# The inverse transforms of two neighbouring tiles, done in a row every second round of the last stage

## The chip, the cores and the metric

The kernel runs on one core of a Trainium2 chip. The metric is the device time of one execution in microseconds. The engines are TensorE (PE in the rows, its weight loads PEld), VectorE (DVE), ScalarE (ACT), GpSimd (POOL) and SyncE (SP), which here only issues transfers.

## What is computed

A block of two layers over x of shape 8 x 2048 x 512, in float32:

```python
proj = (layernorm(x) @ in_proj_w + in_proj_b).reshape(B, L, C, 3)
v, x_branches = proj[..., 0], [proj[..., 1], proj[..., 2]]
v = depthwise_conv3(v) + short_b
h = gelu(gelu(pos @ fw1 + fb1) @ fw2 + fb2)
coefs = (h @ fw3 + fb3).reshape(L, C, 2)
for i in range(2):                       # only the last pass reaches the output
    conv = irfft(rfft(v, n=2*L) * rfft(coefs[..., i], n=2*L))[:L]
    output = x_branches[i] * conv
x = x + output @ out_w + out_b
x = x + layernorm(x) @ (sum_k weights[k] * W[ids[k]]).T + bias
```

The transforms run as products with constant matrices.

## The kernel before

Four stages follow one another: prep builds the filter's first transform step, front does the first layer norm, the projections and the first transform step of each batch, middle the inner transforms and the product with the filter's spectrum, and back the rest. The change is in back, which runs from near 1512 us to the end.

back handles 128 tiles of 128 rows by 512 channels: 8 batches (b) of 16 tiles (t). For each tile TensorE does

- conv: the last inverse step, `psC` from `fin` (loaded from spec3) and the constant `s4`. It is two float32 matmuls, h = 0 and 1, each with 64 output columns of weights, written to the lower and the upper half of psC's partitions. The trace has two records (passes) for each, so four a tile.
- turn_o: four transposes of o into `psP`.
- project: 12 matmuls into `psO` (high and low parts of o times out_w).
- turn_z: four transposes of the normalised rows z into `psT`.
- adapt: 12 matmuls into `psF` (high and low parts of z times the mixed adapter).

VectorE does gate (psC plus a correction, then times the gate, giving `o`), o_low (low part of o), residual (`y` = psO + x, bn_stats, bn_aggr), z_low, finish (psF + yb) and bias_x (out_b added to x). ScalarE makes the high parts and the norm, GpSimd the norm's scalars, `yb` and the correction `corr` in two operations (L1170, L1172). SyncE issues the loads: load_conv, load_gate, load_x.

The order is written by hand with the helper pipelined: each engine has a list of (step, lag), and in round s it runs, in the order of the list, each step for tile s - lag. Rounds run over all tiles of all batches; the first 5 and the last 5 are not full. TensorE's list is [(conv, 1), (adapt, 5), (turn_o, 1), (turn_z, 4), (project, 2)], VectorE's is [(residual, 3), (gate, 1), (finish, 5), (o_low, 1), (z_low, 4), (bias_x, 0)], GpSimd's [(scalars, 3), (bias_y, 3), (correct, 0)], ScalarE's [(norm, 3), (o_high, 1), (z_high, 4), (store, 6)], SyncE's all have lag 0. A tile's conv at lag 1 therefore runs in the same round as its gate, its turn_o and its o_low.

Of the waits that matter here: conv of tile t waits for fin's load and for gate's sum of tile t-2 (psC has two buffers, by t % 2); load_conv of tile t waits for conv of t-2; gate waits for corr and for conv; turn_o for o, and for o_low of the tile before (psP has one buffer); adapt for z_low of the round before; residual for project's psO.

Of the kernel before, what the change touches and what calls it, by code (L numbers as in the profile page):

```python
# [14 lines left out]
B = 8  # L15
# [6 lines left out]
T = 16  # L22
# [110 lines left out]
def pipelined(eng, outer, tiles, stages):  # L133

    fill = max(lag for _, lag in stages)

    def step(i, s, last):
        for stage, lag in stages:
            t = s - lag
            if t >= tiles and not last:  # L140
                stage(i + 1, t - tiles)
            elif 0 <= t < tiles:
                stage(i, t)

    for s in range(fill):
        step(0, s, False)

    def one_pass(i, last):
        for s in range(fill, tiles + fill):
            step(i, s, last)  # L150

    one_pass(0, False)
    with eng.Fori(1, outer - 1) as i:
        one_pass(i, False)
    one_pass(outer - 1, True)


def old(b, t, n):

    return not (isinstance(b, int) and b * T + t < n)  # L160


def hyena_adapter_kernel(nc, x, in_w, in_b, short_w, short_b, fw1, fb1, fw2, fb2, fw3, fb3,
# [14 lines left out]
    def mm3(pe, out_ps, w_hi, w_lo, d_hi, d_lo, first, last):  # L178

        pe.matmul(out_ps, w_hi, d_hi, start=first, stop=False)  # L180
        pe.matmul(out_ps, w_hi, d_lo, start=False, stop=False)  # L181
        return pe.matmul(out_ps, w_lo, d_hi, start=False, stop=last)  # L182
# [861 lines left out]
    def back(bc):  # L1044
        with ExitStack() as st:
# [68 lines left out]
            def no(b, t):  # L1114
                return b * T + t

            @block.sync
            def _(sp):
                def load_edges(b, t):
                    if not (isinstance(b, int) and b == 0):  # L1120
                        return
                    for q in range(2):
                        sp.dma_start(edge[:, q, t], edge_f[q][:, t * C:(t + 1) * C]).then_inc(edge_in[t], 16)  # L1123

                def load_conv(b, t):
                    if old(b, t, 2):
                        sp.wait_ge(c_ps, no(b, t) - 1)
                    sp.dma_start(fin[:, t % 2], spec3[b].rearrange("(r h t) c -> t r h c", h=2, t=T)[t]).then_inc(f_in[t % 2], 16)

                def load_gate(b, t):  # L1130
                    if old(b, t, 2):
                        sp.wait_ge(o_done, no(b, t) - 1)
                    sp.dma_start(gin[:, t % 2], gate_d[b, t // SUB].rearrange("p (s c) -> s p c", s=SUB)[t % SUB]).then_inc(g_in[t % 2], 16)

                def load_x(b, t):
                    if old(b, t, D):
                        sp.wait_ge(y_done, no(b, t) - D + 1)
                    for h in range(2):
                        sp.dma_start(xin[h * N1:(h + 1) * N1, t % D], by_tile(x[b])[h, :, t]).then_inc(x_in[t % D], 16)  # L1139

                pipelined(sp, B, T, [(load_conv, 0), (load_edges, 0), (load_gate, 0), (load_x, 0)])
# [70 lines left out]
            @block.tensor  # L1212
            def _(pe):
                def conv(b, t):
                    pe.wait_ge(f_in[t % 2], 16 * (b * (T // 2) + t // 2 + 1))
                    if old(b, t, 2):
                        pe.wait_ge(a_done, no(b, t) - 1)
                    for h in range(2):
                        mm = pe.matmul(psC[t % 2][h * N1:(h + 1) * N1, :], s4[:, h * T + t, :], fin[:, t % 2, h, :], start=True, stop=True)  # L1219
                    mm.then_inc(c_ps, 1)  # L1220

                def turn_o(b, t):
                    pe.wait_ge(o_done, no(b, t) + 1)
                    if old(b, t, 1):
                        pe.wait_ge(o_lo, no(b, t))
                    for ct in range(CT):
                        mm = pe.transpose(psP[:, ct * P:(ct + 1) * P], o[:, t % 2, ct * P:(ct + 1) * P], ident[:])  # L1227
                    mm.then_inc(p_ps, 1)

                def project(b, t):  # L1230
                    pe.wait_ge(o_lo, no(b, t) + 1)
                    if old(b, t, 2):
                        pe.wait_ge(y_done, no(b, t) - 1)
                    for ct in range(CT):
                        mm = mm3(pe, psO[t % 2][:], oh[:, t % 2, ct * P:(ct + 1) * P], ol[:, t % 2, ct * P:(ct + 1) * P],
                                 woh[:, ct], wol[:, ct], ct == 0, ct == CT - 1)
                    mm.then_inc(o_ps, 1)

                def turn_z(b, t):
                    pe.wait_ge(z_done, no(b, t) + 1)  # L1240
                    if old(b, t, 1):
                        pe.wait_ge(z_lo, no(b, t))
                    for ct in range(CT):
                        mm = pe.transpose(psT[:, ct * P:(ct + 1) * P], z[:, t % 2, ct * P:(ct + 1) * P], ident[:])  # L1244
                    mm.then_inc(t_ps, 1)

                def adapt(b, t):
                    pe.wait_ge(z_lo, no(b, t) + 1)
                    if old(b, t, 2):
                        pe.wait_ge(res_done, no(b, t) - 1)  # L1250
                    for ct in range(CT):
                        mm = mm3(pe, psF[t % 2][:], zh[:, t % 2, ct * P:(ct + 1) * P], zl[:, t % 2, ct * P:(ct + 1) * P],
                                 wfh[:, ct], wfl[:, ct], ct == 0, ct == CT - 1)
                    mm.then_inc(ff_ps, 1)

                pipelined(pe, B, T, [(conv, 1), (adapt, 5), (turn_o, 1), (turn_z, 4), (project, 2)])

            @block.vector
            def _(dve):
# [100 lines left out]
```

## Time and profile before

| what | us |
|---|---|
| median of 3 runs | 2512.56 (2511.91 to 2514.34) |
| the profiled execution | 2518.87 |
| its span, first to last instruction | 2516.8 |
| TensorE busy in the span | 2386.8 (95%) |
| VectorE busy | 1556.8 (62%) |
| GpSimd busy | 914.8 (36%) |
| ScalarE busy | 847.5 (34%) |
| mean granted clock of TensorE | 0.977 of 2.4 GHz |

Shares of the span are averages over stages with different limits. In the last stage, from 1512 us on, TensorE's digits are at 9 tenths or more and VectorE's at 8. Matmuls are pipelined and the ends of their records are modelled, so starts say more than ends: the distance from one start to the next is what a matmul takes in the flow.

### The profile page before, as it was taken

How to read it: one execution, taken by the hardware profiler on the slowest of the kernel's cores; microseconds unless marked ns; L12 is line 12 of the kernel's file. 1: busy time of each engine (PE TensorE's matmuls, PEld its weight loads, DVE VectorE, ACT ScalarE, POOL GpSimd, SP SyncE). 2: the span in 40 equal slices, each digit the busy share in tenths (PEclk: the TensorE clock that was granted, in tenths of full speed). 3: DMA queues.
4: the chain of work that ended last, by engine and by line, in shares of the span. 5: the costliest groups of instructions: out<-in, count | busy, mean ns of one | idle time of the engine just before them, and what ended most of it. 6: DMA issues, size and time to landing. Idle time of an engine off the chain costs nothing. (4 is left out here: it accounts for less than half of the span.)

```text
span 2516.8 us, 39567 instructions
## 1 busy us (share of the span) xinstructions
PE 2386.8 (95%) x12804; PEld 1573.6 (63%) x12804; DVE 1556.8 (62%) x2188; ACT 847.5 (34%) x1151; POOL 914.8 (36%) x1189
## 2 busy tenths in 40 slices
PE   6689999999999999779999987999999999999998
PEld 2257777777777777533333335777777777777776
DVE  6734444443444444257666765788888888888885
ACT  3333344344443344234444441222222222222222
POOL 2322222222222222100000005666666666666664
PEclk9889999999999999889999998999999999999999
DMA  5534435444354435489999987755555555555553
GB/s 188 201 127 151 155 134 190 164 154 168 136 188 150 154 133 191 167 323 346 338 336 339 345 308 236 233 176 171 169 175 175 170 170 174 175 168 170 175 176 94
DMA packets 207925, 496.59 MB, mean 197 GB/s; under 512 B 18411, under 2 KB 18732, under 8 KB 190836
## 3 DMA queue, kind: packets, MB, share of 16 engines
q1 hardware_dynamic: 153588, 395.09, 48.3%
q10 hardware_dynamic: 54272, 100.68, 10.9%
q8 instruction: 35, 0.57, 0.1%
q14 instruction: 30, 0.25, 0.0%
HBM read 276.27 MB, written 219.43 MB: 197 GB/s over the span
## 5 line engine op out<-in xcount | busy, mean ns | idle before, releaser
L1034 DVE TENSOR_TENSOR m_m<-m_psA,m_spec 128x1024 f32<-128x1024 f32 x256 | 295.4, 1217 | 151.9 <-PE m_psA L939 148.4
L1194 ACT ACTIVATE b_z<-b_y,b_shift,b_rstd 128x512 f32<-128x512 f32 x128 | 104.5, 816 | 712.5 <-POOL b_shift L1161 712.5
L701 POOL TENSOR_TENSOR vl<-v,vh 128x512 fp32r<-128x512 f32 x128 | 165.6, 1294 | 433.2 <-ACT vh L661 433.2
L956 PE MATMUL m_psW<-m_m,mats 64*64 64x512 f32 x2048 | 248.6, 592 | 0.0
L939 PE MATMUL m_psA<-m_xin,mats 64*64 64x512 f32 x1536 | 203.3, 604 | 44.6 <-DMA m_xin<-spec 33.8
L180 PE MATMUL b_psF<-wfh,b_zh 128*128 128x512 f32 x512 | 216.3, 423 | 3.4 <-DVE b_zl L1297 3.4
L180 PE MATMUL psV<-wvh,nth 128*128 128x512 f32 x512 | 215.8, 421 | 0.0
L790 DVE TENSOR_TENSOR gto<-psG,bgr 128x512 f32<-128x512 f32 x128 | 87.5, 683 | 204.2 <-PE psG L182 204.2
L180 PE MATMUL b_psO<-woh,b_oh 128*128 128x512 f32 x512 | 212.8, 416 | 0.0
L180 PE MATMUL psG<-wgh,nth 128*128 128x512 f32 x512 | 204.3, 399 | 0.0
L182 PE MATMUL b_psF<-wfh,b_zl 128*128 128x512 f32 x512 | 202.8, 396 | 0.0
L181 PE MATMUL b_psF<-wfl,b_zh 128*128 128x512 f32 x512 | 202.4, 395 | 0.0
L669 ACT ACTIVATE fs1o<-psS 128x1024 f32<-128x1024 f32 x128 | 131.7, 1029 | 209.1 <-PE psS L743 209.1
L182 PE MATMUL psG<-wgh,ntl 128*128 128x512 f32 x512 | 202.1, 395 | 0.0
L181 PE MATMUL psV<-wvl,nth 128*128 128x512 f32 x512 | 201.9, 394 | 0.0
L182 PE MATMUL psV<-wvh,ntl 128*128 128x512 f32 x512 | 201.7, 394 | 0.0
L182 PE MATMUL b_psO<-woh,b_ol 128*128 128x512 f32 x512 | 201.2, 393 | 0.0
L181 PE MATMUL psG<-wgl,nth 128*128 128x512 f32 x512 | 200.7, 392 | 0.0
L181 PE MATMUL b_psO<-wol,b_oh 128*128 128x512 f32 x512 | 200.7, 392 | 0.0
L996 ACT ACTIVATE m_wo<-m_psW 128x1024 f32<-128x1024 f32 x128 | 131.1, 1024 | 201.3 <-PE m_psW L956 201.1
L771 DVE TENSOR_TENSOR ntl<-psT,nth 128x512 fp32r<-128x512 f32 x128 | 88.5, 692 | 175.7 <-ACT nth L655 175.7
L661 ACT ACTIVATE vh<-v 128x512 fp32r<-128x512 f32 x128 | 81.0, 632 | 335.8 <-DVE v L783 335.8
(122 smaller groups left out, 4621.5 us busy)
## 6 DMA issues: line engine op xcount, KB each, us to landing
m_xin<-spec SPq DMA_DIRECT2D x31, 2304.0 KB, 14.8
spec<-fs1o SPq DMA_DIRECT2D x32, 2048.0 KB, 6.8
spec<-m_wo ACTq DMA_DIRECT2D x64, 1024.0 KB, 10.1
b_fin<-spec SPq DMA_DIRECT2D x128, 512.0 KB, 3.9
xg<-in_L_attn_x_dram SPq DMA_DIRECT2D x64, 512.0 KB, 6.2
gate_d<-gto SPq DMA_DIRECT2D x32, 1024.0 KB, 3.9
b_gin<-gate_d SPq DMA_DIRECT2D x128, 256.0 KB, 4.1
b_xin<-in_L_attn_x_dram SPq DMA_DIRECT2D x256, 128.0 KB, 3.5
```

The lines of the kernel that those rows point to most:

```text
L180: pe.matmul(out_ps, w_hi, d_hi, start=first, stop=False)
L181: pe.matmul(out_ps, w_hi, d_lo, start=False, stop=False)
L182: return pe.matmul(out_ps, w_lo, d_hi, start=False, stop=last)
L669: act.activation(s1o[:, slot, :, t % SUB], psS[:], ACT.Copy).then_inc(s_out, 1)
L701: pool.tensor_tensor(vl[:, t % 2], v[:, t % 2], vh[:, t % 2].bitcast(F32), ALU.subtract).then_inc(v_lo, 1)
L771: dve.tensor_tensor(ntl[:, t % 2], psT[t % 2][:].rearrange("p (k r) -> p k r", k=CT), nth[:, t % 2].bitcast(F32), ALU.subtract).then_inc(n ...
L790: dve.tensor_tensor(gto[:, slot, t % SUB], psG[t % 2][:], bgr[:], ALU.add).then_inc(g_out, 1)
L939: mm = pe.matmul(psA[k % RA][half[q], slot, :], w[half[slot]], xin[half[slot], par, B if k < 2 else 2 * (k - 2) + q, :], start=True, stop= ...
L956: mm = pe.matmul(psW[pair % 2][half[slot], q, :], ws[slot][half[q]], m[half[q], pair % RM, part, slot, :], start=part == 0, stop=part == 1)
L996: act.activation(wo[:, par, 2 * pair:2 * pair + 2, :], psW[pair % 2][:], ACT.Copy).then_inc(w_out, 1)
L1034: dve.tensor_tensor(m[:, (k - 2) % RM, part], psA[k % RA][:], spec[:, par, part], ALU.mult).then_inc(m_done, 1)
L1194: act.activation(z[:, t % 2], y[:, t % 2], ACT.Identity, bias=shift[:, t % 2:t % 2 + 1], scale=rstd[:, t % 2:t % 2 + 1]).then_inc(z_done, 1)
```

## The change

conv is no longer called for tile s-1 in each round s. A new step conv_pair has lag 0 and does nothing for an even tile; for an odd tile t it calls conv for t-1 and then for t. So in an odd round s TensorE transforms tiles s-1 and s, in an even round none. The even tiles keep their place, the odd ones move from the head of round t+1 to the head of round t. Which matmuls run, with what data, is as before, and no other engine's list changes.

```diff
+                def conv_pair(b, t):
+
+                    if t % 2:
+                        conv(b, t - 1)
+                        conv(b, t)
+
...
-                pipelined(pe, B, T, [(conv, 1), (adapt, 5), (turn_o, 1), (turn_z, 4), (project, 2)])
+                pipelined(pe, B, T, [(conv_pair, 0), (adapt, 5), (turn_o, 1), (turn_z, 4), (project, 2)])
```

TensorE's order at the head of an odd round (even buffers psO0, psC0 and psF0), end of project to start of adapt, before:

```order
L180 MATMUL b_psO0<-woh,b_oh 128x512
L181 MATMUL b_psO0<-wol,b_oh 128x512
L182 MATMUL b_psO0<-woh,b_ol 128x512
L1219 MATMUL b_psC0<-b_fin,b_s4 64x512 x2
L180 MATMUL b_psF0<-wfh,b_zh 128x512
L181 MATMUL b_psF0<-wfl,b_zh 128x512
```

and now:

```order
L180 MATMUL b_psO0<-woh,b_oh 128x512
L181 MATMUL b_psO0<-wol,b_oh 128x512
L182 MATMUL b_psO0<-woh,b_ol 128x512
L1219 MATMUL b_psC0<-b_fin,b_s4 64x512 x2
L1219 MATMUL b_psC1<-b_fin,b_s4 64x512 x2
L180 MATMUL b_psF0<-wfh,b_zh 128x512
L181 MATMUL b_psF0<-wfl,b_zh 128x512
```

The odd tile's transform (psC1) now stands behind the even tile's.

TensorE's order at the head of an even round (psO1, psC1, psF1), before:

```order
L181 MATMUL b_psO1<-wol,b_oh 128x512
L182 MATMUL b_psO1<-woh,b_ol 128x512
L1219 MATMUL b_psC1<-b_fin,b_s4 64x512 x2
L180 MATMUL b_psF1<-wfh,b_zh 128x512
L181 MATMUL b_psF1<-wfl,b_zh 128x512
```

and now:

```order
L181 MATMUL b_psO1<-wol,b_oh 128x512
L182 MATMUL b_psO1<-woh,b_ol 128x512
L180 MATMUL b_psF1<-wfh,b_zh 128x512
L181 MATMUL b_psF1<-wfl,b_zh 128x512
```

project runs straight into adapt there; the twelve products of adapt and then turn_o follow as before.

## Rows read from the trace of the kernel before

**Rows 1.** Busy time by stretch: PE, PEld, DVE, ACT, POOL, granted clock, DMA share, GB/s.

```profile
2000.00:2100.00 100.00, 100.00 (x477) 71.57 (x477) 82.03 (x118) 25.21 (x41) 67.51 (x92) 1.00 0.57 174
```

**Rows 2.** Waits from 1600 us on: us in total, times, longest us.

```profile
DVE b_res L1304 <- PE b_psF L182: 81.3, 121, 4.7
...
DVE b_o L1273 <- DVE b_corr L1268: 9.9, 48, 0.2
...
PEld b_psP L1227 <- DVE b_o L1273: 2.9, 15, 0.2
```

**Rows 3.** TensorE's timeline, one full round: start us, duration us, instructions [idle before].

```profile
2000.30 0.60 PE L1227 MATMUL b_psP<-b_ident,b_o 128*128 128x128 f32 x4
...
2003.68 0.39 PE L182 MATMUL b_psO<-woh,b_ol 128*128 128x512 f32 x1
2003.99 1.08 PE L1219 MATMUL b_psC<-b_fin,b_s 128*64 128x512 f32 x4
2005.01 0.50 PE L180 MATMUL b_psF<-wfh,b_zh 128*128 128x512 f32 x1
2005.35 0.39 PE L181 MATMUL b_psF<-wfl,b_zh 128*128 128x512 f32 x1
...
2007.91 0.60 PE L1227 MATMUL b_psP<-b_ident,b_o 128*128 128x128 f32 x4
```

**Rows 4.** TensorE's timeline, project to adapt in a late round without a conv.

```profile
2491.48 0.40 PE L182 MATMUL b_psO<-woh,b_ol 128*128 128x512 f32 x1
...
2491.71 0.39 PE L180 MATMUL b_psF<-wfh,b_zh 128*128 128x512 f32 x1
...
2491.94 0.40 PE L181 MATMUL b_psF<-wfl,b_zh 128*128 128x512 f32 x1
```

**Rows 5.** TensorE's timeline in the middle stage, blocks of 64 by 64.

```profile
1120.48 2.07 PE L939 MATMUL m_psA<-m_xin,mats 64*64 64x512 f32 x16
1122.20 2.07 PE L956 MATMUL m_psW<-m_m,mats 64*64 64x512 f32 x16
```

**Rows 6.** Timelines of TensorE and VectorE, from one turn_o to the next o.

```profile
1702.99 0.60 PE L1227 MATMUL b_psP<-b_ident,b_o 128*128 128x128 f32 x4
...
1704.26 0.69 DVE L1277 TENSOR_TENSOR b_ol<-b_psP,b_oh 128x512 fp32r<-128x512 f32 x1 [0.28 <-ACT b_oh L1188]
...
1705.46 0.68 DVE L1262 TENSOR_TENSOR b_xin<-b_xin,bor 128x512 f32<-128x512 f32 x1
1706.81 0.69 DVE L1285 TENSOR_TENSOR b_y<-b_psO,b_xin 128x512 f32<-128x512 f32 x1 [0.66 <-PE b_psO L182]
...
1708.41 0.18 DVE L1293 BATCH_NORM_AGGREGATE b_mv<-b_stats 128x2 f32<-128x6 f32 x1 [0.18 <-DVE b_stats L1287]
...
1709.32 0.69 DVE L1273 TENSOR_TENSOR b_o<-b_corr,b_gin 128x512 f32<-128x512 f32 x1
```

**Rows 7.** Timelines of GpSimd and VectorE, the same round and the one from 2007.91.

```profile
1705.47 1.82 POOL L1172 TENSOR_TENSOR b_corr<-b_edge,b_corr 128x512 f32<-128x512 f32 x1
...
2010.13 1.29 POOL L1172 TENSOR_TENSOR b_corr<-b_edge,b_corr 128x512 f32<-128x512 f32 x1
...
2010.46 1.51 DVE L1262 TENSOR_TENSOR b_xin<-b_xin,bor 128x512 f32<-128x512 f32 x1
...
2014.39 0.69 DVE L1273 TENSOR_TENSOR b_o<-b_corr,b_gin 128x512 f32<-128x512 f32 x1
```

**Rows 8.** Timeline of the stage's start: turn_o behind a wait, twice, and its release.

```profile
1534.74 1.12 PE L1227 MATMUL b_psP<-b_ident,b_o 128*128 128x128 f32 x4 [2.18 <-DVE b_o L1273]
...
1542.08 0.69 DVE L1273 TENSOR_TENSOR b_o<-b_corr,b_gin 128x512 f32<-128x512 f32 x1
...
1542.83 0.66 PE L1227 MATMUL b_psP<-b_ident,b_o 128*128 128x128 f32 x4 [2.21 <-DVE b_o L1273]
```

**Rows 9.** The stage's first conv, its next load's issue, and the first turn_o; the page's loads.

```profile
1512.52 0.60 SPq L1128 DMA_DIRECT2D b_fin<-spec  x1
...
1512.75 1.97 PE L1219 MATMUL b_psC<-b_fin,b_s 128*64 128x512 f32 x4 [11.14 <-DMA b_fin<-spec]
...
1519.26 1.12 PE L1227 MATMUL b_psP<-b_ident,b_o 128*128 128x128 f32 x4 [4.54 <-DVE b_o L1273]
...
b_fin<-spec SPq DMA_DIRECT2D x128, 512.0 KB, 3.9
```

## Prediction

> **What bounds the kernel now.** I read the last stage first, since only it is touched. The busy times by stretch say that TensorE has work in flight for the whole of the stretch, at full clock (1.00, the 2.4 GHz level), while VectorE is busy 82% of it [rows 1]. That alone would make every microsecond taken off TensorE a gain. The table of waits says how near the second engine is: VectorE waits for TensorE's adapter product 81.3 us in 121 rounds, some 0.7 us a round, and in 15 rounds it is TensorE's weight load for turn_o that waits, up to 0.2 us, for VectorE's b_o [rows 2]. So two loops of nearly the same length run side by side, and VectorE's slack is the number that decides this case.
>
> TensorE's round, read from its timeline [rows 3]: turn_o begins at 2000.30, the last product of project at 2003.68, the inverse transform (conv) at 2003.99, adapt at 2005.01 and 2005.35, the next turn_o at 2007.91. The round is 7.61 us. From the start of the last project product to the start of adapt's second product are 1.67 us. In the drained end of the stage, where no conv stands between them, the same way takes 0.46 us (2491.48 to 2491.94) [rows 4]. One conv therefore costs 1.21 us in place. Its streaming is less: in the middle stage sixteen such passes of 512 columns, on four 64 by 64 blocks at once, take 1.72 us from start to start [rows 5], that is 0.43 us a pass. A conv is two matmuls of two passes each, on two column halves at once, so 2 x 0.43 = 0.86 us. The other 0.35 us are the way in and the way out of the half-width form.
>
> VectorE's loop runs from one turn_o to the o that the next turn_o needs [rows 6]: turn_o starts at 1702.99, o_low at 1704.26 (after ScalarE's copy), z_low, bias_x at 1705.46, the residual sum b_y at 1706.81 after a wait of 0.66 us for project's last product, the statistics, bn_aggr at 1708.41, gate's sum, and gate's product at 1709.32, which ends at 1710.01. That is 7.02 us. This round is a short one: bias_x took 0.68 us, because it began before GpSimd's second correction, which then took 1.82 us. In the round from 2007.91 the correction began at 2010.13, before bias_x at 2010.46, and bias_x took 1.51 us; gate's product began at 2014.39, 6.48 us after turn_o, and its end by the same 0.69 us gives 7.17 us [rows 7]. In neither round can b_y start before project has ended, 3.82 us after turn_o (1702.99 to 1706.81). So the loop has a floor of about 7.0 us which no slack on TensorE lowers.
>
> **The change part by part.** Call a round odd when it has both convs (tiles s-1 and s) and even when it has none.
>
> 1. The odd round. The even tile's conv stands where it stood. The odd tile's conv follows it in the same half-width form, so I charge streaming alone: 0.86 us, with 1.02 us as the high bound (2003.99 to 2005.01 in [rows 3], as if TensorE drained between tiles too). TensorE from turn_o to turn_o: 7.61 + 0.86 = 8.47 us.
> 2. The even round. project runs into adapt without a switch: 7.61 - 1.21 = 6.40 us on TensorE.
> 3. Who ends last in each. In the odd round VectorE's 7.0 to 7.4 us are covered by TensorE's 8.47: gate's sum needs the even tile's conv, the first of the two, which ends where it does today, near 2005.07 in [rows 3]; b_y starts some 0.4 us after project's last product does, and gate's sum not before bn_aggr, 1.6 us later (1706.81 to 1708.41). The second conv delays adapt by 0.86 us, and VectorE only waits that much longer for finish. In the even round turn_o is up after 6.40 us, and o is there after 7.0 at the least. Tile s-1's transform was done a whole round earlier, but that frees nothing, because gate stands behind residual in VectorE's order, and residual behind project of the round before. TensorE waits 0.6 us or more in front of turn_o; turn_z, project and the next conv pair are queued behind it. Neither engine's order can make use of the time.
> 4. The price of that wait's end. In rounds that stalled, TensorE started at once with the release (0.06 us), and turn_o's four matmuls took 0.66 us in place of 0.60, as their weights were no longer loaded ahead [rows 8]. I add 0.07 us for the release and 0.06 us for the load.
> 5. The even round's length. What lengthens it today is the second correction on GpSimd, which began 2.22 us after turn_o (2010.13) and held bias_x back [rows 7]. It hangs on the b_y of the round before; behind an odd round that is 0.86 us longer it lies earlier against turn_o by up to as much, bias_x is done sooner, and b_y falls to its floor. I take 7.00 us. The bounds are 6.95 us (the floor with every gap closed) and 7.37 us: the 7.17 of [rows 7] with the 0.2 us wait inside gate that 48 rounds show [rows 2].
> 6. Per pair of rounds: 8.47 + 0.06 + 7.00 + 0.07 = 15.60 us against 2 x 7.61 = 15.22 us, so +0.38 us. From round 5 on, where adapt has begun, to round 128 there are 124 rounds, 62 pairs: +24 us. Low: 8.47 + 6.95 + 0.06 = 15.48, +0.26, +16 us. High: 8.63 + 0.06 + 7.37 + 0.07 = 16.13, +0.91, +56 us; both bounds at once are unlikely, and halfway up from the forecast, +40 us, is about as far as I take the range.
> 7. The start of the stage. The conv of tile 1 now stands ahead of turn_o of tile 0. Its load is issued at 1512.52 and lands in the usual 3.9 us, near 1516.4; conv at the low clock took 1.97 us, so it ends by 1518.4, before turn_o's release at 1519.26 [rows 9]. It is hidden. The next rounds stall 2 us on VectorE anyway, which covers a second conv. I count nothing, plus or minus 2 us.
> 8. SyncE's queue: load_conv of tile t waits for conv of t-2, which is now done at the same place or a round earlier, so each load goes out no later than today. The psC banks and o's buffers ask for steps that lie a round back. Nothing new waits there.
>
> The trace shows the 0.35 us around each conv [rows 3 to 5]. The Trainium skill, TensorEngine Tiling, section Key Properties, says that changing the tiling mode, and not just the tile, drains TensorE. By that rule alone the change removes 62 drains and must gain, which is the first rival below. The trace agrees that the switch costs time; what it speaks against is that this time would reach the end of the kernel.
>
> **The rivals.**
>
> *The saved switches come through.* If o could be ready after 6.40 us, each pair would take 7.61 + 0.86 + 6.40 = 14.87 us, 0.35 us less than 15.22, and 62 pairs give -22 us: 2491 us. For it: TensorE is full [rows 1], and VectorE is busy only 82%. Against it: the chain from turn_o to o takes 7.02 us even in a short round [rows 6], and b_y cannot start before project ends. I give it 8%.
>
> *The two cancel.* Break-even is where the even round takes 15.22 - 8.47 = 6.75 us with the release and the load, so VectorE's loop would need 6.6 us. No round that I read comes to that. 5%.
>
> *The clock falls.* The wait of 0.6 us comes once in two rounds. If TensorE fell to 1.2 GHz behind it, turn_o would take 1.12 us in place of 0.66, as it did after one stall of 2.18 us, while after another of 2.21 us it stayed at 0.66 [rows 8]; project would then double as well, and b_y with it, 2.8 us more for its twelve products of 0.23 us, near +170 us. The waits here are a quarter of either, so 2%.
>
> *VectorE's loop is long in every even round*, since the corrections collide with bias_x as they mostly do now: 7.2 to 7.4 us, +36 to +49 us, 2549 to 2562 us. 15%. This shares my mechanism and only its size is other.
>
> **How the numbers follow.** Forecast (70%): VectorE's loop sets the even rounds at its floor, +24 us. The profiled execution took 2518.87 us around its span of 2516.8, which is 6.3 us above the median of 2512.56; the difference is carried over as it is, so 2512.6 + 24 = 2536.6 us, and the profiled one would be near 2543. The range goes from 2522 us (the low bound of +16 with the start's 2 us and 4 us for a loop slightly better than any row) to 2556 us (past +40). A measurement tells some 0.2% (5 us) from no change. Faster by more than that: 0.08. Within: 0.05. Slower: 0.87.
>
> **What would show it.** In the changed kernel's timeline, turn_o to turn_o should alternate between about 7.1 us and 8.5 us. In the table of waits, TensorE's weight load of b_psP should wait for b_o in about 62 rounds, 0.6 to 0.7 us each, where it was 15 rounds of 0.2. VectorE's wait for b_psF should grow in odd rounds and vanish in even ones. The idle time before conv's and adapt's weight loads should be found half as often. I am wrong if turn_o does not wait (then the loop is shorter than I read it), if the second conv costs over 1 us (then it drains between tiles too), or if the granted clock leaves 1.00.

## Result and profile after

| kernel | median us | ratio to before, 95% interval |
|---|---|---|
| before | 2513.45 (2511.91 to 2517.73) | |
| changed | 2541.35 (2534.86 to 2543.14) | 1.0104 (1.0081 to 1.0126) |

The change makes the kernel 1.0% slower: 28 us between the medians, 26 us by the ratio. Forecast were +24 us and 2536.6 us. The profiled execution's span is 2541.3 us, against 2516.8.

TensorE's timeline of the changed kernel over one odd and one even round (start us, duration us, instruction, idle before; turn_o is L1233 here, turn_z L1250). It answers [rows 3]:

```profile
1999.75 1.94 PE L1219 MATMUL b_psC<-b_fin,b_s 128*64 128x512 f32 x8
2001.62 0.50 PE L180 MATMUL b_psF<-wfh,b_zh 128*128 128x512 f32 x1
...
2004.53 0.60 PE L1233 MATMUL b_psP<-b_ident,b_o 128*128 128x128 f32 x4
...
2007.94 0.40 PE L182 MATMUL b_psO<-woh,b_ol 128*128 128x512 f32 x1
2008.17 0.39 PE L180 MATMUL b_psF<-wfh,b_zh 128*128 128x512 f32 x1
2008.41 0.40 PE L181 MATMUL b_psF<-wfl,b_zh 128*128 128x512 f32 x1
...
2011.63 0.66 PE L1233 MATMUL b_psP<-b_ident,b_o 128*128 128x128 f32 x4 [0.50 <-DVE b_o L1279]
...
2015.42 1.94 PE L1219 MATMUL b_psC<-b_fin,b_s 128*64 128x512 f32 x8
...
2020.19 0.60 PE L1233 MATMUL b_psP<-b_ident,b_o 128*128 128x128 f32 x4
```

From turn_o at 2004.53 to the next at 2011.63 is the even round, 7.10 us; from there to 2020.19 the odd one, 8.56 us. A pair is 15.66 us in place of 2 x 7.61 = 15.22 (in the mean over the stage, from 1560 to 2480 us, the two rounds of a pair are 7.10 and 8.56 us, and a round of the kernel before is 7.62). The even round has no conv and no switch (2007.94, 2008.17, 2008.41 come as closely as in [rows 4]), and yet TensorE stops in front of turn_o, for b_o.

VectorE's timeline over the same even round, which answers [rows 6] and [rows 7]:

```profile
2005.79 0.69 DVE L1283 TENSOR_TENSOR b_ol<-b_psP,b_oh 128x512 fp32r<-128x512 f32 x1 [0.37 <-ACT b_oh L1188]
...
2007.00 0.69 DVE L1268 TENSOR_TENSOR b_xin<-b_xin,bor 128x512 f32<-128x512 f32 x1
2008.37 0.69 DVE L1291 TENSOR_TENSOR b_y<-b_psO,b_xin 128x512 f32<-128x512 f32 x1 [0.68 <-PE b_psO L182]
2009.10 0.69 DVE L1293 BATCH_NORM_STATS2 b_stats<-b_y 128x6 f32<-128x512 f32 x1
2009.97 0.18 DVE L1299 BATCH_NORM_AGGREGATE b_mv<-b_stats 128x2 f32<-128x6 f32 x1 [0.18 <-DVE b_stats L1293]
2010.15 0.69 DVE L1274 TENSOR_TENSOR b_corr<-b_psC,b_corr 128x512 f32<-128x512 f32 x1
2010.88 0.69 DVE L1279 TENSOR_TENSOR b_o<-b_corr,b_gin 128x512 f32<-128x512 f32 x1
```

b_y waits 0.68 us for project and starts 3.84 us after turn_o, its floor. From there VectorE has nothing to wait for but its own results: 3.20 us to the end of b_o at 2011.57, and turn_o starts at 2011.63.

The waits of the changed kernel from 1600 us on (us in total, times, longest), against [rows 2]:

```profile
DVE b_res L1310 <- PE b_psF L182: 88.2, 56, 4.7
DVE b_y L1291 <- PE b_psO L182: 72.7, 113, 1.2
...
PEld b_psP L1233 <- DVE b_o L1279: 54.7, 59, 1.3
PEld b_psC L1219 <- issue: 53.5, 174, 0.4
PEld b_psF L180 <- issue: 47.1, 58, 0.8
PE b_psP L1233 <- DVE b_o L1279: 29.5, 59, 0.9
```

The weight load's wait for b_o has gone from 15 times and 2.9 us to 59 times and 54.7 us.

### The profile page after: what moved, and what is told of

The parts are those of the page before. It is cut to its first block and busy times, and to the rows that moved or that the text cites. A ratio compares the mean times of both kernels' runs of the same rounds, so it can differ in the third digit from the quotient of the medians.

```text
span 2541.3 us, 39567 instructions
## 1 busy us (share of the span) xinstructions
PE 2381.2 (94%) x12804; PEld 1583.5 (62%) x12804; DVE 1472.4 (58%) x2188; ACT 842.6 (33%) x1151; POOL 937.6 (37%) x1189
## 5 line engine op out<-in xcount | busy, mean ns | idle before, releaser
L180 PE MATMUL b_psF<-wfh,b_zh 128*128 128x512 f32 x512 | 209.9, 410 | 3.4 <-DVE b_zl L1303 3.4
L1172 POOL TENSOR_TENSOR b_corr<-b_edge,b_corr 128x512 f32<-128x512 f32 x128 | 195.1, 1524 | 10.0
```

What stands on the lines that cost most here:

```text
L1172: pool.tensor_tensor(corr[:, t % 2], edge[:, 1, t], corr[:, t % 2], ALU.subtract).then_inc(corr_done, 1)
```

## The experiments

All ratios are to the kernel before, run on the same chip. The ten kernels ran on three chips; where medians are given, that of the kernel before on the same chip stands with them.

### Is it the path behind b_y? half_stats and its control

```diff
-                    dve.bn_stats(stats[:], y[:, t % 2]).then_inc(bn_step, 1)
+                    dve.bn_stats(stats[:], y[:, t % 2, 0:C // 2]).then_inc(bn_step, 1)
```

> The changed kernel with one edit: VectorE's bn_stats reads 256 of the 512 channels (so the norm's statistics come from half of each row). It takes time out of the path from project's end to the next o, and nothing out of TensorE. Theory (that path, about 3.2 us behind b_y, sets the even rounds, which are 7.10 us where TensorE needs 6.40): bn_stats falls from 0.70 us to about 0.43, each even round gets 0.27 us shorter, 62 of them give -17 us against the changed kernel, so about +9 us against the kernel before. Rival (the second transform in a row is what costs, or its loads): no change against the changed kernel, +26 us against before.

Measured: 2521.87 us against 2514.74, ratio 1.0034 (1.0025 to 1.0044), which is +9 us. VectorE's timeline of this kernel in an even round:

```profile
2009.81 0.69 DVE L1291 TENSOR_TENSOR b_y<-b_psO,b_xin 128x512 f32<-128x512 f32 x1 [0.61 <-PE b_psO L182]
2010.54 0.43 DVE L1293 BATCH_NORM_STATS2 b_stats<-b_y 128x6 f32<-128x256 f32 x1
```

and TensorE's turn_o around it:

```profile
2005.97 0.60 PE L1233 MATMUL b_psP<-b_ident,b_o 128*128 128x128 f32 x4
...
2012.80 0.66 PE L1233 MATMUL b_psP<-b_ident,b_o 128*128 128x128 f32 x4 [0.23 <-DVE b_o L1279]
```

bn_stats lost 0.26 us (0.69 to 0.43) and the even round lost 0.27 (7.10 to 6.83).

> The kernel before with bn_stats over 256 of the 512 channels (statistics from half of each row), the control of half_stats. Theory: before the change TensorE's 7.61 us bound every round and VectorE's path of 7.0 to 7.5 us is hidden, so the 0.27 us are worth nothing: 0 to -3 us against the kernel before (the 15 short waits of turn_o go). Rival (a shorter bn_stats helps by itself, in whatever kernel): -17 us here too.

Measured: 2513.74 us against 2517.38, ratio 0.9988 (0.9977 to 1.0000). The same 0.26 us an operation, in 128 tiles, are worth about 3 us where TensorE bounds the round, which is hardly told from nothing (the interval ends at 1.0000). In the changed kernel they are worth near 17 us (1.0104 to 1.0034), though there only every second tile counts.

### Or VectorE's load as a whole? no_bias

```diff
-                    dve.tensor_tensor(xin[:, t % D], xin[:, t % D], bor[:], ALU.add).then_inc(xb_done, 1)
+                    dve.sem_inc(xb_done, 1)
```

> The changed kernel with bias_x left out (out_b is not added; VectorE only signals). It takes the longest VectorE operation of a round, 0.7 to 1.5 us, out, but one that stands ahead of project's end. Theory (only what is behind project's last product counts): b_y cannot start earlier, 3.85 us after turn_o as now, so 0 to -3 us against the changed kernel, +23 to +26 us against before. Rival (VectorE's total load of some 6.5 us a round, or its collisions with GpSimd, sets the even rounds): 0.7 us or more off each even round, -43 us against the changed kernel or down to TensorE's bound, near -18 us against before.

Measured: 2536.65 us against 2514.74, ratio 1.0090 (1.0073 to 1.0107), +23 us. VectorE's timeline in an even round, and turn_o's:

```profile
2014.13 0.68 DVE L1303 TENSOR_TENSOR b_zl<-b_psT,b_zh 128x512 fp32r<-128x512 f32 x1
2016.02 0.69 DVE L1291 TENSOR_TENSOR b_y<-b_psO,b_xin 128x512 f32<-128x512 f32 x1 [1.21 <-PE b_psO L182]
```

```profile
2012.17 0.60 PE L1233 MATMUL b_psP<-b_ident,b_o 128*128 128x128 f32 x4
...
2019.27 0.66 PE L1233 MATMUL b_psP<-b_ident,b_o 128*128 128x128 f32 x4 [0.50 <-DVE b_o L1279]
```

bias_x is gone, b_y waits 1.21 us for project in place of 0.68, starts 3.85 us after turn_o all the same, and the even round is again 7.10 us. Work that stands ahead of project's end is worth nothing here; VectorE's load as a whole is not the cause.

### Can the saved switches be had? pair_late and single_late

The statistics (bn_stats and bn_aggr, until now the second half of residual) become a step of their own and leave the place between b_y and gate, and the two engines that follow them make room:

```diff
+                def statistics(b, t):
...
-                pipelined(dve, B, T, [(residual, 3), (gate, 1), (finish, 5), (o_low, 1), (z_low, 4), (bias_x, 0)])
+                pipelined(dve, B, T, [(residual, 3), (gate, 1), (statistics, 3), (finish, 5), (o_low, 1), (z_low, 4), (bias_x, 0)])
...
-                pipelined(act, B, T, [(norm, 3), (o_high, 1), (z_high, 4), (store, 6)])
+                pipelined(act, B, T, [(o_high, 1), (z_high, 4), (norm, 3), (store, 6)])
...
-                pipelined(pool, B, T, [(scalars, 3), (bias_y, 3), (correct, 0)])
+                pipelined(pool, B, T, [(correct, 0), (scalars, 3), (bias_y, 3)])
```

> The changed kernel with bn_stats and bn_aggr moved behind gate in VectorE's list, as a step of its own at lag 3, so that they no longer stand between b_y and gate; ScalarE's norm goes behind o_high and z_high, and GpSimd's correct ahead of scalars, so that the later statistics hold neither back. All of the reference is computed. Theory: the path behind b_y falls from 3.2 us to about 2.2, o is ready 6.1 us after turn_o, before TensorE's 6.40, and TensorE is the bound in both rounds: 8.56 + 6.40 = 14.96 us a pair against 15.25 before, -18 us against the kernel before, -44 against the changed one; turn_o no longer waits for o. Rival (the gap behind the even rounds is not VectorE's order): +26 us against before as now. A third: the later statistics make turn_z or the norm late, which would show as TensorE waiting for b_z.

Measured: 2492.21 us against 2514.74, ratio 0.9914 (0.9897 to 0.9930), -22 us. TensorE's timeline of pair_late:

```profile
2001.21 1.94 PE L1219 MATMUL b_psC<-b_fin,b_s 128*64 128x512 f32 x8
...
2005.99 0.60 PE L1233 MATMUL b_psP<-b_ident,b_o 128*128 128x128 f32 x4
...
2012.43 0.60 PE L1233 MATMUL b_psP<-b_ident,b_o 128*128 128x128 f32 x4
...
2016.14 1.94 PE L1219 MATMUL b_psC<-b_fin,b_s 128*64 128x512 f32 x8
```

The even round takes 6.44 us, turn_o waits for nothing and takes 0.60 us. From pair to pair (2001.21 to 2016.14) are 14.93 us, 0.29 less than 15.22; 62 pairs give 18 us, and the interval of the ratio reaches from 18 to 26 us.

> The kernel before with the same three moves in the lists of VectorE, ScalarE and GpSimd, and conv in each round. It shows what the new orders bring alone. Theory: TensorE already bounds each round at 7.61 us, so only the 15 short waits of 0.2 us go: 0 to -3 us against the kernel before. Rival (the new orders themselves bring the gain of pair_late): -15 us or more.

Measured: 2512.79 us against 2514.74, ratio 0.9990 (0.9980 to 0.9999), -3 us. The new orders alone bring next to nothing, pairing alone costs 26 us, both together gain 22.

### Which of the moves is needed? pair_orders, pair_late_dve, pair_late_act

pair_orders is the changed kernel with the last two changes of the diff (ScalarE's and GpSimd's lists), pair_late_dve with VectorE's alone, pair_late_act with VectorE's and ScalarE's.

> The changed kernel with only the two side moves of pair_late: ScalarE's norm behind o_high and z_high, GpSimd's correct ahead of scalars; VectorE's list as in the changed kernel. Theory: the path from b_y over the statistics and gate to o is untouched, so the even rounds stay at 7.10 us and the time at +24 to +28 us against the kernel before. Rival (the side moves, not the statistics' place, brought pair_late's gain): below the kernel before.

Measured: 2536.73 us against 2516.30, ratio 1.0089 (1.0072 to 1.0106). The side moves are worth nothing by themselves.

> The changed kernel with only the statistics moved behind gate on VectorE; ScalarE and GpSimd in their old order. Theory: bn_aggr ends 1.4 us later, near 7.0 us after turn_o, and z is done 2.5 us behind it. ScalarE's o_high of an even round stands behind that norm in its list and would start at 9.6 in place of 7.1 us after the turn_o before; o_low, z_low, bias_x and b_y follow it. So the gain moves into a wait of ScalarE: each pair near 8.56 + 7.8 = 16.4 us, +60 to +75 us against the kernel before. Rival (ScalarE has room, since it is busy a third of the time): the same gain as pair_late, -20 us.

Measured: 2595.68 us against 2516.30, ratio 1.0321 (1.0303 to 1.0338), +81 us, somewhat more than expected. ScalarE's and TensorE's timelines show the queue of it:

```profile
2005.13 0.82 ACT L1194 ACTIVATE b_z<-b_y,b_shift,b_rstd 128x512 f32<-128x512 f32 x1 [6.81 <-POOL b_shift L1161]
2005.85 0.58 ACT L1188 ACTIVATE b_oh<-b_psP 128x512 fp32r<-128x512 f32 x1
```

```profile
2002.87 0.66 PE L1233 MATMUL b_psP<-b_ident,b_o 128*128 128x128 f32 x4 [0.60 <-DVE b_o L1279]
```

turn_o started at 2002.87, so its copy b_oh could have run from near 2003.5; it stood behind the norm and ran at 2005.85. ScalarE is busy 192.91 of the 900 us from 1600 to 2500 us, and VectorE still waits for it in nearly every round. It isn't alone, though. The waits of pair_late_dve from 1600 us on:

```profile
DVE b_ol L1283 <- ACT b_oh L1188: 237.0, 117, 2.1
...
DVE b_corr L1274 <- POOL b_corr L1172: 55.7, 96, 0.6
```

The second line is a wait for the correction, which GpSimd still makes behind the norm's scalars here. So the +81 us hold two queues, ScalarE's and GpSimd's; the next run has GpSimd's without ScalarE's.

> pair_late without its move on GpSimd (correct stays behind scalars and bias_y). Theory: the correction of tile s then ends about 12.6 us after the turn_o of round s-1, and gate wants it at 11.0 us where round s is even and 13.1 us where it is odd. The 1.6 us that are missing fall into the long rounds, which have 2 us of room, so -16 to -22 us against the kernel before, as pair_late. If GpSimd's place matters after all, it shows as VectorE's b_corr waiting in front of short rounds, and a time between pair_late and the changed kernel.

Measured: 2569.57 us against 2516.30, ratio 1.0211 (1.0194 to 1.0228), +53 us where I had expected -16 to -22. The waits of pair_late_act from 1600 us on:

```profile
DVE b_corr L1274 <- POOL b_corr L1172: 206.2, 116, 1.9
```

and, from the timelines of VectorE and of GpSimd, one turn of the loop behind it:

```profile
2006.98 0.18 DVE L1301 BATCH_NORM_AGGREGATE b_mv<-b_stats 128x2 f32<-128x6 f32 x1 [0.18 <-DVE b_stats L1295]
...
2012.79 0.69 DVE L1274 TENSOR_TENSOR b_corr<-b_psC,b_corr 128x512 f32<-128x512 f32 x1 [1.92 <-POOL b_corr L1172]
...
2015.16 0.18 DVE L1301 BATCH_NORM_AGGREGATE b_mv<-b_stats 128x2 f32<-128x6 f32 x1 [0.18 <-DVE b_stats L1295]
```

```profile
2007.24 0.19 POOL L1156 TENSOR_TENSOR b_rstd<-b_mv,b_eps 128x1 f32<-128x1 f32 x1 [2.50 <-DVE b_mv L1301]
...
2009.67 1.73 POOL L1170 TENSOR_TENSOR b_corr<-b_edge,b_v 128x512 f32<-128x512 f32 x1
2011.48 1.28 POOL L1172 TENSOR_TENSOR b_corr<-b_edge,b_corr 128x512 f32<-128x512 f32 x1
```

I had asked only whether one late correction fits into the next long round. But with the statistics behind gate, the correction waits (in GpSimd's queue) for the statistics, the statistics (in VectorE's) for gate, and gate for the correction: a ring, once a tile, with no long round to give way. One turn is 8.18 us here (2006.98 to 2015.16), more than the 7.47 us that half a pair takes in pair_late. GpSimd is busy two thirds of the time in that stage. The same ring is closed in pair_late_dve. What ScalarE's queue costs where GpSimd's order has been changed, no run shows.

### Another way to the same gain: pair_gate_first

```diff
-                pipelined(dve, B, T, [(residual, 3), (gate, 1), (finish, 5), (o_low, 1), (z_low, 4), (bias_x, 0)])
+                pipelined(dve, B, T, [(gate, 1), (residual, 3), (finish, 5), (o_low, 1), (z_low, 4), (bias_x, 0)])
```

with the moves on ScalarE and GpSimd as in pair_late.

> The changed kernel with gate ahead of all of residual in VectorE's list, and the side moves on ScalarE and GpSimd. In an even round gate's transform is a round old, so it can run before project has ended and o is ready near 4.8 us after turn_o; in an odd one it waits for the even tile's conv, 4.7 us after turn_o, with o near 6.2 us. Theory: TensorE bounds both rounds, 14.93 us a pair as in pair_late, -18 to -22 us against the kernel before. If the wait for conv in the odd rounds holds residual back so far that the next adapt or project waits, the time lies above pair_late by that wait.

Measured: 2490.47 us against 2516.30, ratio 0.9897 (0.9880 to 0.9913), -26 us. TensorE's turn_o in it:

```profile
2002.85 0.60 PE L1233 MATMUL b_psP<-b_ident,b_o 128*128 128x128 f32 x4
...
2011.34 0.60 PE L1233 MATMUL b_psP<-b_ident,b_o 128*128 128x128 f32 x4
...
2017.79 0.60 PE L1233 MATMUL b_psP<-b_ident,b_o 128*128 128x128 f32 x4
```

8.49 and 6.45 us, the same rounds as in pair_late; its interval and pair_late's overlap, so which of them is faster stays open. Both beat the kernel before and the changed one.

### Once more

> The changed kernel unedited, once more beside the kernel before. Theory: ratio 1.010 as measured first (+26 us), rounds of 8.56 and 7.10 us. If a chip alone had made the first difference, it lies elsewhere.

Measured: 2542.12 us against 2517.38, ratio 1.0112 (1.0091 to 1.0133). The loss is there again.

## Why the prediction was right, by its steps

**The bound.** Right: TensorE and VectorE ran side by side with some 0.4 us between them, and the change put 0.86 us into the rounds where TensorE is late anyway. It took 1.2 us of TensorE's work out of the others, of which 0.51 us reached the time (7.61 to 7.10), because there VectorE is next. half_stats, no_bias and pair_late show it from three sides.

**Step 1, the odd round.** 8.47 us forecast (8.53 with step 4's load), 8.56 measured. The second conv in a row costs 0.85 us: 2001.62 - 1999.75 = 1.87 us from the first conv to adapt, against 1.02 in [rows 3]. That is the streaming of its passes and no more, as charged.

**Step 2, TensorE's need in the even round.** 6.40 us; the changed kernel cannot show it, pair_late does: 6.44.

**Steps 3 to 5, the even round.** 7.00 + 0.07 us, measured 7.10. b_y fell to its floor, as said. GpSimd's timeline of that round has the second correction 1.31 us after turn_o, in place of 2.22:

```profile
2005.84 1.30 POOL L1172 TENSOR_TENSOR b_corr<-b_edge,b_corr 128x512 f32<-128x512 f32 x1
```

It is all but through when bias_x starts, at 2007.00, and bias_x takes 0.69 us. The turn_o behind the wait takes 0.66 us. Two terms were a little small: the floor is 3.84 us and not 3.82, and the wait that I took as "0.6 us or more" is 0.66 (7.10 - 6.44); the 0.50 us in TensorE's row count from the modelled end of its last matmul.

**Step 6, the sum.** +0.38 us a pair forecast, +0.44 measured (15.66 - 15.22; +0.42 against the mean round of 7.62). 62 pairs: 24 us and 27 us. By the traces the stage grew from 1004.0 us (1512.75 to 2516.8) to 1029.4 (1511.94 to 2541.3), by 25 us, and that is all of the difference: the stages before it took 0.8 us less.

**Step 7, the start.** The result held, its working did not. TensorE's timeline:

```profile
1511.94 1.97 PE L1219 MATMUL b_psC<-b_fin,b_s 128*64 128x512 f32 x4 [10.86 <-DMA b_fin<-spec]
1517.75 1.98 PE L1219 MATMUL b_psC<-b_fin,b_s 128*64 128x512 f32 x4 [3.84 <-DMA b_fin<-spec]
1519.66 1.12 PE L1233 MATMUL b_psP<-b_ident,b_o 128*128 128x128 f32 x4
1524.29 0.85 PE L1233 MATMUL b_psP<-b_ident,b_o 128*128 128x128 f32 x4 [3.52 <-DVE b_o L1279]
```

The load of tile 1 did not land in the median's 3.9 us: it was issued at 1511.70, among the stage's first loads, and released its conv 6.05 us later. That conv held turn_o up: 7.72 us after the first conv in place of 6.51 [rows 9]. It was not hidden, but by the second turn_o it was made good. At the sixth turn_o (1557.46 us, and 1558.14 in the kernel before) the two kernels stand 45.52 and 45.39 us behind their first conv, so the start gave and cost next to nothing.

**Step 8, the loads.** Right: from 1600 us on no wait of TensorE for a load of b_fin is in the table, though the median from issue to landing has grown from 3.9 to 4.7 us.

**The rivals.** The saved switches did not come through, but they exist: pair_late had them, 18 us by its trace. The Trainium skill, TensorEngine Tiling (Array Packing), section Key Properties, says that a change of the tiling mode drains TensorE. The trace agrees that the switch has a price, 0.35 us; the rule does not say whether that reaches the end. VectorE's loop wasn't long in every even round either: the mean is 7.10 us, near the floor. The clock stayed: from 1550 to 2500 us the granted clock of the changed kernel is 1.00, the 2.4 GHz level, and over the whole kernel it is 0.979, 0.977 before.

**What was to be seen.** The rounds alternate, 59 waits of turn_o stand where 62 were said (the window leaves some out), finish waits 56 times in place of 121. The weight load's wait was larger than the 0.6 to 0.7 us said, 0.93 us in the mean (54.7 us in 59 waits); the matmul's own, in the last row of the table, is 0.50 us. One sign was wrong: the idle time before conv's weight loads was to be found half as often and is found 174 times in place of 117. Within a pair of convs two later groups of loads (2000.23 and 2000.66 us in the pair from 1999.75) come while passes stream, each after 0.28 us of idle weight path. They count as idle, three times a pair in all, though they hold nothing up: the pair takes the 1.87 us of step 1. Before adapt's loads it is half, 58 times.

## What to carry to other kernels

When two engines take turns and have rounds of nearly the same length, look at evenness before looking at savings. Here a saving that made one engine's rounds uneven was paid for in the long rounds and lost in the short ones, until the other engine's path was cut to fit into the shortest (pair_late, pair_gate_first). Before moving work between rounds, take the time from the first engine's release to the moment that the second gives it back, and compare it with the short round and not with the mean. If it does not fit, cut what stands between the late product and the result that is waited for (here 1.0 us of statistics that nobody needed yet), and then follow each queue that the moved step stands in, for rings as well as for single delays.

## What I had not expected of the hardware

The changed kernel keeps VectorE less busy and is slower. bias_x reads two operands from SBUF, as the corrections on GpSimd do. VectorE's groups of the last stage, before and then after (mean ns of one behind the busy time):

```profile
L1262 DVE TENSOR_TENSOR b_xin<-b_xin,bor 128x512 f32<-128x512 f32 x128 | 183.6, 1434 | 10.2 <-DMA b_xin<-in_L_attn_x_dram 10.2
```

```profile
L1268 DVE TENSOR_TENSOR b_xin<-b_xin,bor 128x512 f32<-128x512 f32 x128 | 99.5, 777 | 8.9 <-DMA b_xin<-in_L_attn_x_dram 8.9
```

Its mean fell from 1.43 to 0.78 us, 84 us in all, with the same data; what changed is its place against GpSimd's operations. In [rows 7] the one or the other of a colliding pair is stretched, to 1.51 or to 1.82 us. no_bias shows the other half: with bias_x left out, GpSimd's second correction is never stretched. Its groups in the last stage of the changed kernel and of no_bias:

```profile
L1172 POOL TENSOR_TENSOR b_corr<-b_edge,b_corr 128x512 f32<-128x512 f32 x128 | 195.1, 1524 | 10.0
```

```profile
L1172 POOL TENSOR_TENSOR b_corr<-b_edge,b_corr 128x512 f32<-128x512 f32 x127 | 164.5, 1295 | 10.0
```

From 1600 to 2500 us it takes 1285 to 1308 ns in no_bias. Since bias_x stands ahead of project's end, none of its 84 us reached the time. The Trainium skill, SBUF — State Buffer, section SBUF: two separate sides, says that a VectorE operation with two SBUF inputs and a GpSimd operation that reads SBUF take the shared port pair in turn, the second blocked for the whole of the first. The stretched pairs and no_bias agree with it, though bias_x's 1.51 us in [rows 7] is 0.13 us less than the 0.96 us that the correction still had to run and its own 0.68 us, an estimate from these rows. No run here took the corrections away and left bias_x.
